# The router logits of the first 128 tokens move from the router loop into four steps of the attention

## The reference, cut to what matters

```python
q, k, v = ...                                      # 16 heads of 16 channels
weights = softmax(einsum('bhqd,bhkd->bhqk', q, k) * scale)
x = x + einsum('bhqk,bhkd->bhqd', weights, v) @ Wo + bo
xn = rmsnorm(layernorm(x), norm_gamma)
sn = rmsnorm(slot_embeds, slot_norm_gamma)
logits = einsum('bnd,esd->bnes', xn, sn)           # 2048 tokens x 1024 slots
dispatch = softmax(logits, over the tokens)
combine = softmax(logits, over the 1024 slots of a token)
slots = einsum('bnd,bnes->besd', xn, dispatch)
...                                                # two layers per expert
out = einsum('bmd,bnm->bnd', eo, combine)
```

## Time and profile before

| | |
|---|---|
| median of 3 runs | 1351.25 us (1350.41 to 1352.27) |
| the profiled execution | 1352.97 us, span 1351.2 us, mean granted clock 0.958 |
| TensorE busy | 1224.3 us of the span (91%) |
| ScalarE busy | 929.5 us (69%) |
| VectorE busy | 744.7 us (55%) |
| attention | from about 682 us to 1096.6 us |
| router loop | 1096.5 us to 1169.6 us |
| column maxima, slots, experts, combination | 1169.6 us to 1351 us |

### The profile page before, as it was taken

The page is one execution under the profiler, slowest core; times in us unless marked ns, Lnnn a source line. Parts: engine busy times, 40 slices in busy tenths (PEclk is TensorE's granted clock), DMA queues, the critical chain, the costliest instruction groups (busy, mean ns, idle before and its releaser), DMA issues.

```text
span 1351.2 us, 19337 instructions
## 1 busy us (share of the span) xinstructions
PE 1224.3 (91%) x7848; PEld 641.3 (47%) x7848; DVE 744.7 (55%) x829; ACT 929.5 (69%) x1213; POOL 384.4 (28%) x280
## 2 busy tenths in 40 slices
PE   8679987998978897899979999999999999999999
PEld 4234543444443453355623333333333345588988
DVE  4999999999999999983352001001001237640011
ACT  5867756677657854662379999999989967742300
POOL 2646766666556765750000000000001000000000
PEclk9789988999988998999979999999999999999999
DMA  6534665243324432449461000000000000203501
GB/s 183 176 110 122 230 219 192 94 152 128 111 86 144 133 131 106 160 151 256 104 166 25 1 2 2 1 2 1 2 2 1 1 32 0 94 1 161 244 16 47
DMA packets 43033, 128.02 MB, mean 95 GB/s; under 512 B 6103, under 2 KB 21400, under 8 KB 39545
## 3 DMA queue, kind: packets, MB, share of 16 engines
q1 hardware_dynamic: 42942, 126.75, 29.0%
HBM read 109.64 MB, written 17.09 MB: 94 GB/s over the span
## 4 chain that ended last, share of the span: by engine, by line
PE 41%; ACT 26%; DVE 22%; issue 9%; DMA 1%; DVEq 0%; SPq 0%; POOL 0%; ACTq 0%
ACT arena L1101 18%; DVE ps L1268 13%; PE ps L2169 4%; PE ps L2300 4%; PE ps L2343 4%; PE ps L2156 4%; PE ps L2228 4%; PE ps L1946 4%; DVE arena L1279 4%; PE ps L2007 3%; PE ps L1992 2%; PE ps L2318 2%; ACT ps L856 2%; PE ps L2331 2%; PE ps L1726 2%
## 5 line engine op out<-in xcount | busy, mean ns | idle before, releaser
L1101 ACT ACTIVATE arena<-ps,bound 128x1536 f32<-128x1536 f32 (+1 forms) x278 | 403.9, 1559 | 13.1 <-PE ps L2156 12.7
L662 POOL TENSOR_TENSOR arena<-arena 128x1024 f32<-128x1024 f32 x127 | 298.3, 2350 | 217.5 <-DVE arena L1279 181.8
L1268 DVE TENSOR_TENSOR_SCAN ps<-ps,arena 128x1024 f32<-128x1024 f32 x128 | 300.6, 2349 | 9.2 <-ACT ps L856 7.8
L2156 PE MATMUL ps<-arena 97*32 97x512 bf16 x3264 | 239.2, 385 | 18.8 <-ACT arena L1101 12.9
L1946 PE MATMUL ps<-arena,ident 128*128 128x512 f32 x512 | 238.3, 611 | 3.9 <-DVE arena L1279 3.9
L2169 PE MATMUL ps<-arena 128*32 128x512 f32 (+1 forms) x1664 | 227.5, 598 | 3.1 <-DVE arena L1587 2.6
L856 ACT ACTIVATE ps<-arena 128x512 f32<-128x512 f32 x256 | 166.2, 682 | 52.0 <-DVE arena L1279 47.6
L2156 PEld LDWEIGHTS ps<-arena 97*32 97x32 bf16 (+1 forms) x3264 | 84.0, 96 | 211.9 <-ACT arena L1101 125.4
L645 POOL TENSOR_TENSOR rstd<-ve,mhalf 128x4 f32<-128x4 f32 (+3 forms) x23 | 25.5, 1110 | 495.7 <-DVE ve L1559 421.5
L1279 DVE TENSOR_TENSOR arena<-ps,arena 128x1024 f32<-128x1024 f32 x128 | 156.0, 1219 | 9.5 <-DMA arena<-bc_scratch 1.9
L1946 PEld LDWEIGHTS ps<-arena,ident 128*128 128x128 f32 x512 | 99.5, 197 | 125.9 <-issue 119.1
(11 more groups left out here) (205 smaller groups left out, 1384.2 us busy)
## 6 DMA issues: line engine op xcount, KB each, us to landing
arena<-bc_scratch SPq DMA_DIRECT2D x128, 512.0 KB, 4.2
arena<-in_mw SPq DMA_DIRECT2D x16, 1024.0 KB, 10.3
qx_scratch<-arena SPq DMA_DIRECT2D x48, 128.0 KB, 3.3
arena<-qx_scratch SPq DMA_DIRECT2D x4, 1536.0 KB
arena<-kx_scratch SPq DMA_DIRECT2D x1, 4803.0 KB
kx_scratch<-arena SPq DMA_DIRECT2D x36, 128.0 KB, 4.7
arena<-vx_scratch SPq DMA_DIRECT2D x1, 3328.0 KB
vx_scratch<-arena SPq DMA_DIRECT2D x6, 512.0 KB, 5.1
```

The lines of the kernel that those rows point to most:

```text
L662: product = pool.tensor_tensor(dbu[:, w % DR], du[:, DP * p:DP * p + DP], over(bg[:, w // BG % 2, n % BG], DP), ALU.mult)
L1101: act.activation(flat(prob[k % PSLOTS])[0:n, 0:w], banks(SPAN * (k % 2), SPAN)[0:n, 0:w], ACT.Exp, bias=bound[0:n, 3:4], scale=HD ** -0.5) ...
L1268: dve.tensor_tensor_scan(decay_banks(w), decay_banks(w), flat(dbu[:, w % DR]), carry[:, DP * p, n:n + 1], ALU.mult, ALU.add).then_inc(S["s ...
L2156: last = mm(ps[r:r + w, SPAN * (k % 2) + s % SPAN, :], kx[0:XR + 1, head, b * P + r:b * P + r + w], qx[0:XR + 1, c, head, :], start=True, ...
```

## The change

The four products of `logits(0, 0)` and `logits(0, 1)` leave the router loop and go one by one into the idle steps 254, 258, 262 and 266, into bank 7: two for the first 512 logits, two for the second. After each two VectorE copies the 512 logits to `lg[:, 0]`; ScalarE's copy of `lg[:, 0]` goes. The waits are counted anew: `l_ps` and `l_copy` count one less, and `snt_ps` and `snt_ready` go on to 6 for the new halves.

```diff
         piece_at[token_step] = "tokens", 0
+        for n in range(4):
+            piece_at[[k for k in idle_steps if k > token_step][n]] = "logits", n
...
-            sp.wait_ge(S["l_ps"], TT)
+            sp.wait_ge(S["l_ps"], TT - 1)
...
             def turned_tokens(t):
                 act.wait_ge(S["xnt_ps"], t + 1)
-                if t >= 2:
-                    act.wait_ge(S["l_ps"], t - 1)
+                if t == 2:
+                    act.wait_ge(S["snt_ps"], 6)
+                if t >= 3:
+                    act.wait_ge(S["l_ps"], t - 2)
...
-                act.wait_ge(S["l_ps"], t + 1)
-                act.activation(lg[:, t], banks(2 * (t % 2), 2), ACT.Copy).then_inc(S["l_copy"], 1)
+                if t:
+                    act.wait_ge(S["l_ps"], t)
+                    act.activation(lg[:, t], banks(2 * (t % 2), 2), ACT.Copy).then_inc(S["l_copy"], 1)
@@ VectorE, out_piece @@
+                elif c == "logits":
+                    n = s // DK
+                    if s % DK == DK - 1:
+                        dve.wait_ge(S["snt_ps"], 5 + n)
+                        dve.tensor_copy(lg[:, 0, 512 * n:512 * n + 512], bank(7)).then_inc(S["snt_ready"], 1)
@@ VectorE, last_run; token_max changes in the same way @@
             def last_run(t):
-                dve.wait_ge(S["l_copy"], t + 1)
+                if t:
+                    dve.wait_ge(S["l_copy"], t)
+                else:
+                    dve.wait_ge(S["snt_ready"], 6)
@@ TensorE, out_piece @@
+                elif c == "logits":
+                    n, k = s // DK, s % DK
+                    if k == 0:
+                        pe.wait_ge(S["snt_ready"], 4 + n)
+                        pe.wait_ge(S["xnt_ready"], 1)
+                    last = mm(bank(7), xnt[:, 0, k], snt[DK * k + n], start=(k == 0), stop=(k == DK - 1))
+                    if k == DK - 1:
+                        last.then_inc(S["snt_ps"], 1)
...
             def turn_tokens(t):
                 if t == 1:
-                    pe.wait_ge(S["xnt_ready"], 1)
+                    pe.wait_ge(S["snt_ready"], 6)
...
             def logits(t, n):
-                    if t >= 2:
-                        pe.wait_ge(S["l_copy"], t - 1)
+                    if t >= 3:
+                        pe.wait_ge(S["l_copy"], t - 2)
...
-            pe.wait_ge(S["snt_ready"], 4)
             for t in range(TT):
...
-                logits(t, 0)
-                logits(t, 1)
+                if t:
+                    logits(t, 0)
+                    logits(t, 1)
```

More of the change, by code:

```diff
@@ L2275, in _ @@
             pe.wait_ge(S["l_run"], TT)
-            pe.wait_ge(S["l_copy"], TT)
+            pe.wait_ge(S["l_copy"], TT - 1)
             turn_maxima(0)
```

## The result

The changed kernel takes 1354.96 us (median of 18 runs) where the kernel before takes 1351.6 us (median of 18); the ratio is 1.0025, 95% interval 1.0018 to 1.0033. It is slower by 0.25%, some 3.4 us. One of the changed kernel's 18 runs was a slow one of 2525.69 us, which the ratio leaves out; the median of the other 17 is 1354.80 us. The profiled execution has a span of 1354.1 us.

The account below looks back on a forecast made before the run. It took ScalarE to bound the late attention, with TensorE close behind, and TensorE alone the router loop from tile 3. Attention +2.4, seam -1.1 and clock +1.6 gave +2.9 on 1351.25: 1354.1 us, range 1351.4 to 1355.5.

Parts of the forecast that it names:

- Attention, +2.4: Late attention: each of four idle steps with a piece takes 1.81 us, so the last `attend` starts 2.4 us later.
- Seam, -1.1: After the last `attend`: 3.44 us of matmuls go, but TensorE waits 2.2 us for VectorE; the gain is 1.1 us.
- Clock, +1.6: Behind the new seam wait: TensorE's clock falls to 0.50, slowing the projection and tile 1's first matmuls, 1.6 us lost.
- The first rival: At the seam: the wait comes but the clock stays up, +1.3 us, 1352.6 us; chance 0.32.
- The one with hidden pieces: In the attention: the pieces hide, +1.2 us or less there, -1.1 at the seam, 1351.3 us; chance 0.08.
- the one with a longer low clock: Behind the seam wait: the low clock stays longer than at step 210, +4.6 us, 1355.9 us; chance 0.10.
- the likeliest case: Attention, seam and clock terms all come: 1354.1 us, own range 1353.4 to 1354.8; chance 0.5.

Follow-up runs that it names:

- e2_add: The kernel before with four added products of 128x128 by 512 columns, results unread, in idle steps 254, 258, 262 and 266; ratio 1.0014 to before.
- e5_remove: The changed kernel without the four products, so tile 0's logits are not computed; ratio 0.9995 to the kernel before.
- e12_remove_look: The kernel of e5_remove, unchanged, profiled a second time; 254.67 us from the last `attend` to the end of the span.
- e1_fill: The changed kernel with four scrap products on TensorE in the wait before the projection; ratio 1.0007 to the kernel before.
- e11_fill_look: The kernel of e1_fill, unchanged, profiled a second time; 254.64 us from the last `attend` to the end of the span.

## Why the prediction came out as it did

**Attention, +2.4.** Measured +2.46 in the profile and +2.47 by e2_add alone. The row that carried it was the output piece with 256 columns: its fixed 0.29 us and twice its columns gave 1.81 us, and the step takes 1.81. ScalarE's lead shows in its first gap, 0.19 us where the other three are 0.27 or 0.28, so it took 0.1 off once there; in A hardly any of it is left (four times 0.62 is 2.48).

The Trainium skill (TensorE: Matmul & The Clock Gate, Part 2, Step-by-step) has weight loads pulled ahead of running matmuls, where the row groups don't conflict or the load goes to the background buffer. Had that hidden these loads, the steps would have been 1.52 us. In no run here is a piece between 32-column tiles as cheap: 1.38 us with 256 columns, 1.81 with 512, the same 0.29 us over, and the PEld rows show the loads at both changes start with their matmuls and not ahead. The measurement decides. The trace puts about 0.10 us at each of three places: before the piece's first matmul (1061.64 instead of 1060.89 + 0.66), between its two (1061.64 to 1062.18, for 0.43) and behind the second (1062.18 to 1062.70, for 0.43). That the late loads are the cause is the likely reading; no run here separates them from anything else that such a change brings.

**Seam, -1.1.** The projection starts 1.08 us sooner behind the last `attend` in the changed kernel (3.62 for 4.70), and E falls by 0.96 to 1.03 us where the clock holds (e5_remove, e12_remove_look, e1_fill, e11_fill_look); the rest is a weight load exposed behind the wait (1.99 us for 1.89), which stood as the lower bound. The 3.44 us taken out were mostly VectorE's cover.

**Clock, +1.6.** E is 256.08 to 256.18 us in the three profiles of the changed kernel and 254.64 to 254.71 where the wait is filled or the clock held: 1.4 to 1.5 us. The mechanism was right, the size within 0.2 us. That the fall came at all had chances of 0.6 in the prediction, taken from one like wait and from counts, with no rule that says when it comes: part of this hit is luck.

**The sum.** 2.46 + 0.50 = +2.96 us in the profile, +2.9 forecast; 1354.96 us measured, 1354.1 forecast. Each term is within 0.2 us; the small misses of the seam (0.1 us gained too much) and of the clock (0.1 us charged too much) cancel. The first rival (no fall, +1.3) is what e1_fill shows by its distances, +2.48 - 1.01 = +1.47; its ratio gives +0.9, so that its median of 1352.62 us equals the rival's 1352.6 is chance. The one with hidden pieces and the one with a longer low clock didn't come. Too cautious was the spread around the likeliest case: I gave 0.58 to no measurable change, and the ratio lies above 0.2% with most of its interval. I took the frequency of the fall from waits all over the program, six of twelve; in the changed kernel it was three profiles of three.

**What stays open.** What decides whether a wait of this length is followed by a fall. The wait's length alone does not, as step 210 and e5_remove show. Its place in time suits all profiles of the changed kernel and of the two without pieces, and so would the fuller attention further back; no run separates them. And some 0.5 us of the 3.4 by the ratio lie outside the stretch that the profile explains, within the interval's width.

## What to carry to other kernels

Before moving work out of a stage, ask what it covers: here 3.44 us of matmuls hid 2.2 us of another engine, and only 1 us was to be had until something else useful took their place. Before moving it into idle slots, measure the slot in time, not by name: the idle step had 0.53 us beside its scores, of which the change of tiles takes 0.29, so two transposes fitted for nothing, half a product cost 0.19 us and a whole one 0.62. A wait on TensorE can be dearer than its length, since the matmuls behind it may run at half the clock; scrap work in the wait made the kernel faster.

## What the runs showed of the hardware

A full-array f32 product between scores on 32-column tiles costs a fixed 0.29 us beside its columns, at 256, 512 and two times 512 columns alike (steps of 1.38, 1.81 and 2.67 us). The weight loads at such a change started with their matmuls, those between 32-column tiles 0.22 us ahead. A wait of 2.17 or 2.18 us on TensorE was followed by a granted clock of 0.50 in four profiles and by none in two, one of 1.91 us in thirteen and by none in one, and one of 0.45 us in none of two. The fall came 1.7 to 1.8 us into the wait of 2.2 us and cost 1.4 to 1.5 us.
